# Maxima read in PSUM and end one-hots made on ScalarE in a four-layer graph network on one core

## What is computed

```python
x = x + gat(h)     # 8 heads: e = leaky(a_s[src]+a_d[dst]); softmax over the edges of a node; weighted sum of xp[src]
x = x + gcn(h)     # sum of x[src] over the edges of a node
x = x + pna(h)     # mean, min, max, sum of squares of m over the edges of a node
x = x + gatv2(h)   # one head: softmax of att . leaky(x_l[src]+x_r[dst]), weighted sum
# pna: m = concat(h[dst], h[src]) @ W_pre + b
#      mean, mn, mx, std = segment_sum(m)/deg, segment_min(m), segment_max(m), sqrt(...)
# gat: p = exp(e - segment_max(e)[dst]); out = segment_sum(p/segment_sum(p)[dst] * xp[src])
```

## Time and profile before

| | |
|---|---|
| median of 3 runs | 5962.01 us (5955.12 to 5962.85) |
| the profiled execution | 5946.32 us, span 5944.5 us |
| busy, share of the span | TensorE 3804.6 us (64%), VectorE 4148.1 us (70%), ScalarE 1470.4 us (25%), GpSimd 3529.3 us (59%) |
| TensorE's granted clock, mean | 0.751 of full speed |
| gathers | 4 x 832 of GpSimd, 942 us busy in the GAT pass, 795 us in the PNA pass |

### The profile page before, as it was taken

The page is one execution under the profiler, slowest core; times in us unless marked ns, Lnnn a source line. Parts: engine busy times, 40 slices in busy tenths (PEclk is TensorE's granted clock), DMA queues, the critical chain, the costliest instruction groups (busy, mean ns, idle before and its releaser), DMA issues. The chain is left out here.

```text
span 5944.5 us, 95091 instructions
## 1 busy us (share of the span) xinstructions
PE 3804.6 (64%) x24005; PEld 3232.3 (54%) x24006; DVE 4148.1 (70%) x8912; ACT 1470.4 (25%) x3477; POOL 3529.3 (59%) x3528
## 2 busy tenths in 40 slices
PE   6366666665233333334688888887494188888886
PEld 5355555554233333324577777777364166666664
DVE  7599999999633333335899999999425266666666
ACT  0233333332000000001233333333111133333332
POOL 1477777774377777762566666664121266766663
PEclk5555555565655556566899999999697589989888
DMA  1233333332122222210222222222000933323322
GB/s 52 56 72 74 74 75 75 75 75 47 34 52 52 52 52 52 52 45 25 80 64 64 64 64 64 64 64 60 14 1 21 32 71 71 71 70 72 70 68 62
DMA packets 331427, 341.81 MB, mean 57 GB/s; under 512 B 186836, under 2 KB 233031, under 8 KB 331332
## 3 DMA queue, kind: packets, MB, share of 16 engines
q0 software_dynamic: 106832, 223.07, 16.4%
q1 hardware_dynamic: 224500, 117.67, 9.8%
HBM read 319.62 MB, written 21.66 MB: 57 GB/s over the span
## 5 line engine op out<-in xcount | busy, mean ns | idle before, releaser
L800 POOL DMA_INDIRECT e_G<-dr_tab,src_idx x832 | 941.5, 1132 | 272.5 <-issue 252.3
L800 POOL DMA_INDIRECT m_G<-dr_tab,src_idx x832 | 795.3, 956 | 490.5 <-PE m_OUT L1805 247.9
L800 POOL DMA_INDIRECT v_G<-dr_tab,src_idx x832 | 811.4, 975 | 448.2 <-issue 224.5
L800 POOL DMA_INDIRECT s_G<-dr_tab,src_idx x832 | 785.2, 944 | 275.3 <-issue 266.1
L1631 PE MATMUL s_OUT<-s_G,s_S 128*128 128x129 f32 x1664 | 390.0, 427 | 733.6 <-DMA s_G<-dr_tab,src_idx 733.6
L1631 PEld LDWEIGHTS s_OUT<-s_G,s_S 128*128 128x128 f32 x1664 | 361.9, 330 | 761.6 <-DMA s_G<-dr_tab,src_idx 678.1
L1604 DVE TENSOR_TENSOR ACC<-ACC,s_OUT 128x129 f32 x832 | 241.5, 290 | 680.6 <-PE s_OUT L1631 576.9
L1735 DVE TENSOR_TENSOR ACC<-ACC,m_OUT 128x512 f32 x832 | 564.5, 678 | 4.1 <-PE m_OUT L1805 3.6
L1804 PE MATMUL m_OUT<-m_XB,m_SE 128*128 128x256 f32 x1664 | 497.4, 381 | 0.0
L1803 PE MATMUL m_OUT<-m_G,m_S 128*128 128x128 f32 x1664 | 360.8, 299 | 196.4 <-DVE m_SE L1743 141.0
L1177 PE MATMUL e_OUT<-e_RH,e_S 128*128 128x145 f32 x1664 | 442.3, 457 | 11.5 <-DVE ACC L987 5.6
(11 more groups left out here) (346 smaller groups left out, 8514.0 us busy)
## 6 DMA issues: line engine op xcount, KB each, us to landing
e_LR<-dr_row_loc SPq DMA_DIRECT2D x104, 256.0 KB, 3.4
m_MS<-dr_row_start SPq DMA_DIRECT2D x104, 256.0 KB, 3.4
v_LR<-dr_row_loc SPq DMA_DIRECT2D x104, 256.0 KB, 3.4
e_G<-dr_tab,src_idx POOLq DMA_INDIRECT x832
s_G<-dr_tab,src_idx POOLq DMA_INDIRECT x832
m_G<-dr_tab,src_idx POOLq DMA_INDIRECT x832
v_G<-dr_tab,src_idx POOLq DMA_INDIRECT x832
dr_tab<-XPA SPq DMA_DIRECT2D x7, 476.0 KB, 3.1
```

Of the source, the lines that this page charges most:

```text
L800: pool.indirect_dma_start(out=out, out_offset=None, in_=table, in_offset=bass.IndirectOffsetOnAxis(ap=g["src_idx"][:, step:step + 1], axis ...
```

## The change

In the GAT pass the forward scan writes its result over the scores in PSUM (`ET`) and the backward scan reads them there; `FW` goes, and a copy keeps the last maximum of a group (`last`). TensorE is released by that copy, not by the scan. The weights go from `RH` to a PSUM bank by a ScalarE copy, and the weighted rows read them there. The test for segment ends is made once for all steps, and the column that counted them goes from `RH` and `ACC` (145 to 144 columns; whether a node has edges is read from its sum of weights). The node one-hots `ST` are made by ScalarE, a square and a rectifier, two groups ahead, between its edge one-hots and the factor. In the PNA pass `SE` is made by ScalarE, a group ahead: a copy of eight columns, eight squares into a bf16 tile, a rectifier; four of the eight one-hot quarters remain on VectorE, behind the first four additions. Declarations of semaphores and unchanged lines are left out.

```diff
@@ -831,7 +831,8 @@
-    self.FW = sb("FW", [heads, 2, SLOTS])
+    self.last = sb("last", [heads, 2])
+    self.SQ = sb("SQ", [P, SLOTS], BF16)
@@ -882,6 +886,7 @@
         wait(sp, self.st_done, k - 1)
+        wait(sp, self.lf_done, k - 1)
         locrow(k, c)
@@ -891,39 +896,50 @@
-    V.memset(self.FW[:, 1, SLOTS - 1:SLOTS], -BIG).then_inc(self.start, 1)
+    V.memset(self.last[:, 1:2], -BIG).then_inc(self.start, 1)
...
-    self.node_slots(dve, 0, 0)
-    self.node_slots(dve, 0, 1)
+    self.first_slots(dve, 0, 0)
+    self.first_slots(dve, 0, 1)
...
-def node_slots(self, dve, i, b):
+def first_slots(self, dve, i, b):
...
-    V.tensor_copy(self.LF[:, c:c + 1], self.LR[0:self.heads, c, 0:1])
-    V.tensor_scalar(self.ST[:, c, :], self.LR[:, c, :], self.g["iota_col"][:], None, ALU.is_equal).then_inc(self.st_done, 1)
-def node_slots_ahead(self, dve, i, b):
-    self.node_slots(dve, i + (b + 2) // 4, (b + 2) % 4)
+    V.tensor_copy(self.LF[:, c:c + 1], self.LR[0:self.heads, c, 0:1]).then_inc(self.lf_done, 1)
+def first_slots_ahead(self, dve, i, b):
+    self.first_slots(dve, i + (b + 2) // 4, (b + 2) % 4)
+def node_slots(self, act, k, i, b, read):
+    c = b % 2
+    wait_alone(act, self.locrow_in[c], 16 * (2 * i + b // 2 + 1), self.stood)
+    if not isinstance(k, int) or k > 0:
+        wait_alone(act, self.st_done, k, self.stood)
+    self.nc.scalar.activation(self.SQ[:], self.LR[:, c, :], ACT.Square, bias=self.g["iota_col"][:], scale=-1.0).then_inc(self.sq_done, 1)
+    wait_alone(act, self.sq_done, k + 1, self.stood)
+    wait_alone(act, read, k - 1, self.stood)
+    self.nc.scalar.activation(self.ST[:, c, :], self.SQ[:], ACT.Relu, bias=self.g["ones"][:, 0:1], scale=-1.0).then_inc(self.st_done, 1)
...
-    FW, CM, drop = self.FW, self.CM, self.drop
+    last, CM, drop = self.last, self.CM, self.drop
...
-    V.tensor_tensor_scan(out=FW[:, p, :], data0=self.MS[:, p, :], data1=self.scores[:],
-                         initial=FW[:, 1 - p, SLOTS - 1:SLOTS], op0=ALU.add, op1=ALU.max).then_inc(self.maxima_step, 1)
-    dve.wait_ge(self.st_done, k + 1)
+    V.tensor_tensor_scan(out=self.ET[:], data0=self.MS[:, p, :], data1=self.ET[:],
+                         initial=last[:, 1 - p:2 - p], op0=ALU.add, op1=ALU.max).then_inc(self.maxima_step, 1)
+    dve.wait_ge(self.lf_done, k + 1)
...
-    V.tensor_tensor_scan(out=CM[:, ::-1], data0=self.ME[:, p, ::-1], data1=FW[:, p, ::-1],
-                         initial=-BIG, op0=ALU.add, op1=ALU.max).then_inc(self.cm_done, 1)
-    dve.wait_ge(self.cm_done, k + 1)
-    V.tensor_tensor(drop[:], FW[:, 1 - p, SLOTS - 1:SLOTS], CM[:, 0:1], ALU.subtract).then_inc(self.maxima_step, 1)
+    V.tensor_tensor_scan(out=CM[:, ::-1], data0=self.ME[:, p, ::-1], data1=self.ET[:, ::-1],
+                         initial=-BIG, op0=ALU.add, op1=ALU.max).then_inc(self.cm_step, 1)
+    V.tensor_copy(last[:, p:p + 1], self.ET[:, SLOTS - 1:SLOTS]).then_inc(self.cm_done, 1)
+    dve.wait_ge(self.cm_step, k + 1)
+    V.tensor_tensor(drop[:], last[:, 1 - p:2 - p], CM[:, 0:1], ALU.subtract).then_inc(self.maxima_step, 1)
@@ -1024,7 +1040,10 @@
+    has = sb("has", [P, SPAD])
...
+    PP = ctx.enter_context(nc.psum_tensor("e0_PP", [P, 512], F32))
+    weight = PP[:, 0:GROUP * heads].rearrange("p (s h) -> p s h", h=heads)
@@ -1051,7 +1070,9 @@
                 wait_alone(act, dif_done, k + 1, parts.stood)
-                nc.scalar.activation(RH[:, b % 2, :, D:D + heads], DIF[:], ACT.Exp).then_inc(parts.p_done, 1)
+                nc.scalar.activation(RH[:, b % 2, :, D:D + heads], DIF[:], ACT.Exp).then_inc(exp_done, 1)
+                wait_alone(act, exp_done, k + 1, parts.stood)
+                nc.scalar.copy(weight, RH[:, b % 2, :, D:D + heads]).then_inc(parts.p_done, 1)
@@ -1070,7 +1091,11 @@
                 onehots(k, b)
+                if not (isinstance(k, int) and k >= GROUPS - 2):
+                    parts.node_slots(act, k + 2, i + (b + 2) // 4, (b + 2) % 4, dp_done)
                 parts.factor(act, k)
+            parts.node_slots(act, 0, 0, 0, dp_done)
+            parts.node_slots(act, 1, 0, 1, dp_done)
             in_groups_of_four(act, body)
@@ -1084,17 +1109,15 @@
             parts.prepare(dve)
+            c.then(V.tensor_scalar(has[:], g["loc_end"][:], 0.0, None, ALU.is_ge))
...
                 V.tensor_tensor(DIF[:], SC[:, p], stab, ALU.subtract).then_inc(dif_done, 1)
-                V.tensor_scalar(RH[:, p, :, AC - 1:AC], g["loc_end"][:, bass.ds(k * GROUP, GROUP)].unsqueeze(2),
-                                0.0, None, ALU.is_ge).then_inc(has_done, 1)
-                dve.wait_ge(has_done, k + 1)
                 V.tensor_tensor(RH[:, p, :, WC:WC + heads], stab,
-                                RH[:, p, :, AC - 1:AC].to_broadcast([P, GROUP, heads]), ALU.mult)
+                                has[:, bass.ds(k * GROUP, GROUP)].unsqueeze(2).to_broadcast([P, GROUP, heads]), ALU.mult)
@@ -1103,7 +1126,7 @@
                                 G[:, b, steps, 0:D].rearrange("p s (h f) -> p s h f", h=heads),
-                                RH[:, b % 2, steps, D:D + heads].unsqueeze(3).to_broadcast([P, GROUP // 4, heads, hd]),
+                                weight[:, steps, :].unsqueeze(3).to_broadcast([P, GROUP // 4, heads, hd]),
                                 ALU.mult).then_inc(rh_done, 1)
@@ -1144,7 +1167,7 @@
-                    parts.node_slots_ahead(dve, i, b)
+                    parts.first_slots_ahead(dve, i, b)
@@ -1179,7 +1202,7 @@
-            pe.wait_ge(split_done, 5)
+            pe.wait_ge(split_done, 6)
@@ -1655,6 +1678,8 @@
+    APART = sb("APART", [P, GROUP, P], BF16)
+    LOC = sb("LOC", [P, GROUP])
@@ -1711,12 +1739,30 @@
+            def end_onehots(k, b):
+                if not is_first(k):
+                    wait_alone(act, apart_done, k, stood)
+                nc.scalar.copy(LOC[:], g["loc_end"][:, bass.ds(k * GROUP, GROUP)]).then_inc(loc_in, 1)
+                wait_alone(act, loc_in, k + 1, stood)
+                if not is_first(k):
+                    wait_alone(act, se_done, k, stood)
+                for s in range(GROUP):
+                    ins = nc.scalar.activation(APART[:, s, :], g["iota_row"][:], ACT.Square, bias=LOC[:, s:s + 1], scale=-1.0)
+                ins.then_inc(apart_done, 1)
+                wait_alone(act, apart_done, k + 1, stood)
+                wait_alone(act, step_done, (k - 1) * GROUP, stood)
+                nc.scalar.activation(SE[:, b % 2], APART[:], ACT.Relu, bias=g["ones"][:, 0:1], scale=-1.0).then_inc(se_done, 1)
             def body(k, i, b):
+                if not is_last(k):
+                    end_onehots(k + 1, b + 1)
                 back(k, i, b)
...
             minus_masks(1, 0, 1)
+            end_onehots(0, 0)
             in_groups_of_four(act, body)
@@ -1736,14 +1782,13 @@
-            def onehots(k, b, which, part):
+            def onehots(k, b, part):
                 n = GROUP // 4
-                out, loc = ((S, g["loc"]), (SE, g["loc_end"]))[which]
-                ins = V.tensor_tensor(out[:, b % 2, part * n:(part + 1) * n], g["iota_row"][:].unsqueeze(1).to_broadcast([P, n, P]),
-                                      loc[:, bass.ds(k * GROUP + part * n, n)].unsqueeze(2).to_broadcast([P, n, P]),
+                ins = V.tensor_tensor(S[:, b % 2, part * n:(part + 1) * n], g["iota_row"][:].unsqueeze(1).to_broadcast([P, n, P]),
+                                      g["loc"][:, bass.ds(k * GROUP + part * n, n)].unsqueeze(2).to_broadcast([P, n, P]),
                                       ALU.is_equal)
-                if which == 1 and part == 3:
+                if part == 3:
                     ins.then_inc(s_done, 1)
@@ -1762,7 +1807,7 @@
                                          initial=XT[:, 1 - c, m, SLOTS - 1:SLOTS], op0=ALU.add, op1=op).then_inc(scanned, 1)
-                between = [lambda w=w, part=part: onehots(k, b, w, part) for part in range(4) for w in range(2)]
+                between = [lambda part=part: onehots(k, b, part) for part in range(4)]
                 if is_first(k):
@@ -1795,6 +1840,7 @@
                 pe.wait_ge(s_done, k + 1)
+                pe.wait_ge(se_done, k + 1)
                 pe.wait_ge(sq_done, k + 1)
@@ -1869,7 +1915,7 @@
                     stores=((g["tab0"], XPA[:, :, 0:D + HEADS], True),))
-    ACC = ctx.enter_context(nc.sbuf_tensor("ACC0", [P, TILES, D + 2 * HEADS + 1], F32))
+    ACC = ctx.enter_context(nc.sbuf_tensor("ACC0", [P, TILES, D + 2 * HEADS], F32))
     gat_pass(nc, g, g["tab0"], XPA[:, :, D + HEADS:D + 2 * HEADS], ACC)
@@ -1901,7 +1947,7 @@
-                c.then(V.tensor_scalar(none[:], ACC[:, :, D + 2 * HEADS], -1.0, BIG, ALU.add, ALU.mult))
+                c.then(V.tensor_scalar(none[:], ACC[:, :, D], 0.5, -BIG, ALU.is_lt, ALU.mult))
                 c.then(V.tensor_tensor(r[:], big, none[:].unsqueeze(2).to_broadcast(th), ALU.add))
```

(8 more changed lines are left out.)

## The result

The kernel after took 6073.71 us in the median of 4 runs (6062.41 to 6076.93), beside 5962.43 for the kernel before on the same chip (5955.12 to 5967.34): a ratio of 1.0193, 95% interval 1.0165 to 1.0221. The forecast was 5937, with a range up to 5976: the sign was wrong, and the time lies outside. The profiled execution is one of 6062.4 us with a span of 6060.6, 116.1 us above the span of before.

What follows compares the result with a forecast made beforehand. VectorE was taken to bound both the GAT and PNA passes. GAT -8 for its groups and -9 for gathers, with PNA -8, gave -25 us, so a median of 5937 from 5962; range 5900 to 5976.

Steps and rivals of the forecast that it cites:

- The sum of ScalarE's chain: PNA pass: ScalarE's new chain takes 12.1 to 12.15 us a group, just under VectorE's 12.16.
- TensorE waiting for the first copy back: PNA pass: a sign that would show the forecast right; the hop to TensorE was put at 0.10 to 0.15 us.
- Rival (A): PNA pass: slower, ScalarE's chain takes VectorE's place; at 12.8 us a group, 6002 us in all; chance 0.12.
- Rival (D): Faster: VectorE or TensorE was slowed too; full clock for GAT transposes saves up to 40 us, about 5897; chance 0.08.
- the removed quarters: PNA pass: four one-hots leave VectorE, additions five to eight come 0.90 us apart; -0.12 us a group, bounds 0 and -1.3.
- The start of the pass: PNA pass: two rounds of one-hots stand ahead of ScalarE's first row squares, partly hidden by VectorE's work; +3 us.
- The term for the test: GAT pass: the per-group test of segment ends leaves VectorE's path behind the hole; -0.21 us a group.
- that for the first gathers: GAT pass: gathers no longer stand still, which gives back VectorE's waits in the first groups; -9 us, ends -10 and 0.
- The steady groups: GAT pass: removed and added work net to -0.08 us a group over 104 groups, -8 us, ends +15 and -20.
- The copy of the last maximum: GAT pass: it stands between the second scan and the transposes' semaphore; +0.08 us a group on the path.
- The second scan: GAT pass: reading PSUM in place of SBUF, it takes 2.33 us against 2.28, +0.05 a group.
- rival (C): GAT pass: PSUM operands cost VectorE, 0.25 us more a group, 5963 us in all, 5972 by the skill's figure; chance 0.05.

Runs made afterwards that it cites:

- the moved one: Kernel after, with ScalarE's PNA end squares put behind its second copy back and the rectifier behind its third: 5893.73 us, 0.9911 of the kernel before.
- filled: Kernel after, with eight products of no use put into TensorE's hole in each PNA group, ScalarE's order kept: 5902.06 us, 0.9923 of the kernel before.

## Why the prediction was wrong

**PNA, the failed step.** The sum of ScalarE's chain took "from the first sum to the last copy 3508.16 - 3503.26 = 4.90" from a profile in which the clock was 1.00, and took no account of the longer hole that the same chain puts in front of that first sum. There TensorE stood 1.39 us; after, it stands 2.17, the clock falls behind that, and the first sum to the last copy takes 6.56; with the hole filled it is 4.91. The text even names "TensorE waiting for the first copy back" among its signs, and prices it with a hop of 0.10 to 0.15 us alone. The rest of that sum was right: 12.1 + (6.56 - 4.90) = 13.76, and the group shown takes 3518.03 - 3504.30 = 13.73; with the hole filled and ScalarE's order kept, the group is 12.02 to 12.09, close under the 12.1 to 12.15 of the text. Rival (A) is what came, with its sign and its place, but its price was argued from hops missed, 0.1 each, and at 12.8 it ended at 6002. Its chance of 0.12 rested on "ACT is at 442 of 1280 us", which says nothing of a chain. Rival (D) named the clock, but as a gain and in the other pass.

**PNA, the removed quarters.** Forecast -0.12 us a group; with the clock kept, the pass of before takes 12.18 a group and the moved one 11.99 (whole kernels, above), -0.19, of which the new order on ScalarE may be a part. Additions five to eight are 0.90 apart, as forecast: of the 4 x 0.34 us taken off VectorE nearly all was in the shadow of the additions. The start of the pass, forecast +3, can't be told apart in -19.4 us from the GAT edit alone to the moved version (4091.1 - 2837.0 against 4071.1 - 2836.4).

**GAT.** Forecast -17, measured -34 by the start of the PNA pass, and 29 us in the whole with the edit alone. The term for the test held (-0.21; 0.18 with it put back), and that for the first gathers nearly (-9; VectorE's waits for rows behind 260 us fell from 9.6 to 3.1). The steady groups, forecast 0.08 shorter, are 0.22 shorter: the forecast put what the gathers give there (0.06) at nothing, and took the added work too dear. Some 4 us of the 34 lie behind the pass's last scan, and no term stood for them. The copy of the last maximum takes 0.12 us, but TensorE begins 2.47 us after the second scan's start, where it was 2.43, so +0.04 for +0.08:

```profile
778.97 2.27 DVE L938 TENSOR_TENSOR_SCAN e_CM<-e_ME,e_ET 8x1024 f32<-8x1024 bf16 x1
...
781.17 0.12 DVE L940 COPY e_last<-e_ET 8x1 f32<-8x1 f32 x1
...
781.44 0.99 PE L1222 MATMUL e_SB<-eye,e_CM 8*128 8x8 f32 x8 [4.11 <-DVE e_last L940]
```

The PSUM operands cost next to nothing:

```profile
L932 DVE TENSOR_TENSOR_SCAN e_ET<-e_MS,e_last,e_ET 8x1024 f32<-8x1024 bf16 x104 | 243.1, 2338 | 0.0
L938 DVE TENSOR_TENSOR_SCAN e_CM<-e_ME,e_ET 8x1024 f32<-8x1024 bf16 x104 | 236.6, 2275 | 3.6
L1127 DVE TENSOR_TENSOR e_RH<-e_G,e_PP 128x256 f32<-128x256 f32 x416 | 172.2, 414 | 0.3 <-ACT e_PP L1075 0.3
```

The second scan reads PSUM in 2.275 us, where it was 2.28 from SBUF, +0.05 was forecast; the first, which now writes PSUM too, takes 2.333 for 2.326 in the median. VectorE waits 0.3 us in all for the copied weights. So rival (C) did not come, and of the added terms that were forecast only the +0.04 is left. The Trainium skill (Perfetto Trace Analysis, Optimizing Scalar/DVE Operations) gives 125 ns of overhead on PSUM for 60 on SBUF. By that figure, the runs disagree: a read costs nothing more (2.275 for 2.28), a write 0.007 us.

**gatv2.** No step of the forecast touched it, and it took 14.5 us more. In the whole kernels its group takes 11.25 to 11.41 us with unchanged code, 11.27 before, 11.35 with the GAT edit alone, 11.30 moved, 11.25 filled, and longer where the mean granted clock of the pass is lower (0.90 at 11.25, 0.88 at 11.41). The filled version has both edits and the time of the kernel before, so neither edit makes it by itself. Each figure is of one execution, and those of the kernel before differ by 37 us on that chip (5935.22 to 5972.63), so it can be chance; what sets it stays open.

## What to carry to other kernels

A chain that sums to just under the bound is not safe: look at what each engine in it does while the chain runs ahead of it, and price TensorE's work behind a lengthened hole at the lower clock as well as at the full one. Work moved to an engine with idle time belongs where that engine waits, not ahead of what others wait for: here the same instructions gave -0.9% in one place and +1.9% in another. That gain holds where gathers are seen complete in time; on two chips where they were not, the moved version was 8.1 and 8.4% slower than the kernel before, and on one of them the GAT edit by itself 5.1%. To tell a clock from a chain, fill the hole with products of no use and see whether the time falls.

## What was not expected of the hardware

A TensorE hole of 2.17 us once a group was followed by 3.4 us at half clock; behind holes of 1.4 and, in the moved version, of 1.70 the clock stayed at 1.00. Whether another loop with such holes keeps its clock is not shown. On three chips of the study gathers were seen complete up to 37 us after their issue, and then a kernel whose gathers run further ahead was slower: 17.0 us a GAT group with them free, 13.4 with them held up by the scan. That the lead itself makes the difference is not shown. On the first chip the lead from the end of a group's last gather instruction to the first use of its rows was 5.3 us in the kernel before and 12.6 after, as a rule with no wait. And the gatv2 pass took 11.64 us a group without its gathers, more than the 11.27 with them, at a clock of 0.84 for 0.90.
